# A three-layer decoder kernel on one core: a new order of the steps around each batch boundary

## What is computed

```python
x = _layernorm(x + _L0_attn_ref(x, ...))                      # no mask; aperture and expression gates
x = _layernorm(x + _L0_xattn_ref(x, ctx, ctx, mask, ...))     # keys and values from ctx, with a mask
x = _layernorm(x + _L0_ffn_ref(x, ...))                       # 16 experts with causal attention
# both attentions, in short, for every head:
scores = (x @ Wq) @ (kv @ Wk).T / sqrt(32)     # 1024 x 1024; masked: -1e9 where mask == 0
out    = softmax(scores) @ (kv @ Wv)
y      = concat(heads of out) @ Wo
```

## Time and profile before

| | |
|---|---|
| Median of 3 runs | 4500.99 us (4493.58 to 4504.22) |
| The profiled execution | 4493.35 us, span 4491.5 us, mean granted TensorE clock 0.964 |
| Span of the two attentions | to about 3512 us |
| Third layer | 3512 to 4491 us |
| PE / DVE / POOL / ACT busy | 4094.5 / 2557.7 / 1800.2 / 1704.6 us |

### The profile page before, as it was taken

One profiled execution on the slowest core, in us unless ns is written; L12 is line 12 of the kernel. 1 busy time (PEld: TensorE's weight loads), 2 busy tenths in 40 slices (PEclk: granted clock), 3 DMA queues, 4 the chain that ended last, 5 costly groups with the idle time before them and its releaser, 6 DMA issues. The chain is left out here.

```text
span 4491.5 us, 65447 instructions
## 1 busy us (share of the span) xinstructions
PE 4094.5 (91%) x20596; PEld 2374.2 (53%) x20596; DVE 2557.7 (57%) x4092; ACT 1704.6 (38%) x3114; POOL 1800.2 (40%) x1263
## 2 busy tenths in 40 slices
PE   4899989989999999899989988998998599999998
PEld 3543744364446436443644364436443477777776
DVE  2564456446534655576567566756674555565554
ACT  1355145425443553344234424442444322222222
POOL 2223122222241224476357535754664244444343
PEclk8999999999998999999999999999999799999998
DMA  2321232132213224322422333223220300000000
GB/s 82 73 50 48 71 93 59 53 85 65 56 51 94 52 62 150 85 43 72 141 67 43 90 127 76 53 94 119 57 43 20 139 27 27 27 29 30 29 29 12
DMA packets 136375, 294.68 MB, mean 66 GB/s; under 512 B 19856, under 2 KB 37904, under 8 KB 136016
## 3 DMA queue, kind: packets, MB, share of 16 engines
q1 hardware_dynamic: 125520, 272.93, 22.5%
q10 hardware_dynamic: 10496, 17.31, 1.1%
HBM read 145.74 MB, written 43.25 MB: 42 GB/s over the span
## 5 line engine op out<-in xcount | busy, mean ns | idle before, releaser
L1133 ACT ACTIVATE probs_a<-half_a 128x512 f32<-128x512 f32 x2048 | 1120.8, 595 | 976.7 <-PE half_a L934 451.0
L931 PE MATMUL half_a<-stack_a 97*128 97x512 f32 x2048 | 874.0, 485 | 75.1 <-DMA stack_a<-mrow_a 36.5
L1369 DVE TENSOR_REDUCE mx_a<-wide_a 128x1 f32<-128x1024 f32 x512 | 601.3, 1219 | 548.3 <-PE wide_a L890 542.3
L1365 DVE CUSTOM_DVE_ANT_0 wide_a<-wide_a,mask_q_a 128x1024 f32<-128x1024 f32 x512 | 619.5, 1245 | 289.3 <-PE wide_a L890 278.4
L890 PE MATMUL wide_a<-stack_a 96*128 96x512 f32 x2048 | 674.3, 438 | 61.3 <-DVE mx_a L1369 31.0
L931 PEld LDWEIGHTS half_a<-stack_a 97*128 97x128 f32 x2048 | 377.3, 194 | 633.1 <-ACT probs_a L1133 326.3
L779 POOL TENSOR_TENSOR psums_a<-psums_a,probs_a 128x1024 f32<-128x1024 f32 x232 | 559.7, 2432 | 144.2 <-ACT probs_a L1133 121.3
L1758 PE MATMUL work_e<-w_in_e,x_e 128*128 128x512 f32 x2304 | 573.9, 401 | 17.7 <-DVEq L2014 10.3
L873 PE MATMUL acc_a<-probs_a,v_a 128*32 128x512 f32 x4096 | 553.0, 610 | 3.1 <-ACT u_a L1104 3.0
L890 PEld LDWEIGHTS wide_a<-stack_a 96*128 96x128 f32 x2048 | 386.0, 196 | 230.7 <-DVE mx_a L1369 57.0
L1758 PEld LDWEIGHTS work_e<-w_in_e,x_e 128*128 128x128 f32 x2304 | 429.7, 191 | 119.4 <-issue 20.3
(11 more groups left out here) (238 smaller groups left out, 4558.9 us busy)
## 6 DMA issues: line engine op xcount, KB each, us to landing
stack_a<-qk_a SPq DMA_DIRECT2D x336, 256.0 KB, 4.9
y_a<-x SPq DMA_DIRECT2D x8, 2048.0 KB, 8.8
x<-y_a SPq DMA_DIRECT2D x8, 2048.0 KB, 7.5
mstage_a<-mask SPq DMA_DIRECT2D x32, 512.0 KB, 4.3
mstage_a<-mask_t SPq DMA_DIRECT2D x32, 512.0 KB, 4.1
stage_a<-x_t SPq DMA_DIRECT2D x24, 512.0 KB, 3.7
stack_a<-first_a SPq DMA_DIRECT2D x48, 256.0 KB, 5.0
x_t<-xts_late_a ACTq DMA_DIRECT2D x10, 1024.0 KB, 7.6
```

The costliest lines, as they stand in the source:

```text
L931: last = pe.matmul(bank[:, :], stack[0:3 * DH + 1, s, 2 + h, kt * P:(kt + 1) * P], stack[0:3 * DH + 1, s, h, c * CH:(c + 1) * CH], start=T ...
L1133: act.activation(probs[:, kt % 2 * 2 + h, c * CH:(c + 1) * CH], bank[:, :], ACT.Exp, scale=SCALE).then_inc(free, 1)
L1365: dve.tensor_tensor_reduce(bank[:, :], bank[:, :], mask_q[:, t, :], 1.0, -3e38, ALU.add, ALU.max, mx[:, p % 3, n:n + 1]).then_inc(free, 1)
L1369: dve.tensor_reduce(mx[:, p % 3, n:n + 1], bank[:, :], AX.X, ALU.max).then_inc(free, 1)
```

## The change

Six edits, all to the order of the steps and to one helper of TensorE:

- `MAXIMA`: no maxima in tile 0 of pair 0; the row becomes 0, 2, 3, 3, 3, 3, 3, 2 (19 instead of 21), and pair 4 gets 3 instead of 2 in tiles 6 and 7.
- `mneg` of a pair is put behind the first two `st` of the next tile, in front of that tile's maxima, where it stood behind the tile's last `st`. In pair 5 it comes at the end of the tile in which the sixteenth maximum stands.
- The masked section's key masks 8 to 15 leave V (one per V tile) and go two at a time behind K(0,0), K(1,0), K(2,0), K(3,0).
- The last pair's norm steps in the masked section: steps 0; 1 and 2; 3 and 4; 5 and 6 behind V tiles 0, 1, 2, 3 instead of one behind each of tiles 1 to 7 (counted from 0, step n behind tile n + 1).
- `with_maxima`: of a unit's maxima all but one stand in front of it, the unit is cut in two halves of 6 matmuls (a step `part` for the first), and the last one stands between them.
- The order of K and Q units and of the transposes around `mneg` 0 changes: the two blocks of the diff with `xt[:2]` and with `xt[:HALF]` are for a next batch with the mask and without it.

```diff
-MAXIMA = ((2, 3, 3, 3, 3, 3, 2, 2),) + ((2,) * 8,) * 4 + ((2, 3, 3, 3, 3, 3, 1, 0), (2, 2, 2, 2, 1, 0, 0, 0), (0,) * 8)
+MAXIMA = ((0, 2, 3, 3, 3, 3, 3, 2),) + ((2,) * 8,) * 3 + ((2, 2, 2, 2, 2, 2, 3, 3),) + ((2, 3, 3, 3, 3, 3, 1, 0), (2, 2, 2, 2, 1, 0, 0, 0), (0,) * 8)
...
-            steps += [("st", p, kt, 0, c) for c in range(NC_)]
-            misc = due
+            steps += [("st", p, kt, 0, c) for c in range(NC_)] + due
...
-                steps += [units_[0], ("st", p, kt, 1, 0), units_[1], ("st", p, kt, 1, 1)] + misc
+                steps += [units_[0], ("st", p, kt, 1, 0), units_[1], ("st", p, kt, 1, 1)]
             else:
-                steps += units_ + [("st", p, kt, 1, c) for c in range(NC_)] + misc
+                steps += units_ + [("st", p, kt, 1, c) for c in range(NC_)]
...
             steps += [("pv", *before, part) for part in parts] + late
+            if p == 5:
+                steps += due
+                due = []
...
-def mask_places():
-
-    place = {("pv", n): n for n in range(4)}
-    place.update({("V", 3 + n): 4 + n for n in range(5)})
-    place.update({("out", 1 + 2 * n): 9 + n for n in range(4)})
-    place.update({("K", n): 13 + n for n in range(3)})
+def mask_places(att):
+
+    if att == 1:
+        return {("K", n // 2): (TT + n, 2) for n in range(0, TT, 2)}
+    place = {("V", 3 + n): (4 + n, 1) for n in range(5)}
+    place.update({("out", 1 + 2 * n): (9 + n, 1) for n in range(4)})
+    place.update({("K", n): (13 + n, 1) for n in range(3)})
...
     def masks(kind, n):
 
-        if change and (kind, n) in mask_at:
-            m = mask_at[kind, n]
-            return [("mask", m)] + ([("mload", m + 2)] if m + 2 < 2 * TT else [])
-        return []
+        if nxt != 1 or (kind, n) not in mask_at:
+            return []
+        from_, count = mask_at[kind, n]
+        return [step for m in range(from_, from_ + count)
+                for step in [("mask", m)] + ([("mload", m + 2)] if m + 2 < 2 * TT else [])]
 
     def with_maxima(units, rates):
 
         out = []
         for unit, rate in zip(units, rates):
-            out.extend(unit)
-            out.extend(first[:rate])
-            del first[:rate]
+            out += first[:rate - 1]
+            del first[:rate - 1]
+            out.append(("part", *unit))
+            out.append(first.pop(0))
+            out.append(unit)
         return out
...
-            tail[n + 1].append(("norm", PAIRS - 1, n))
+            tail[(n + 1) // 2 + (1 if att == 0 else 0)].append(("norm", PAIRS - 1, n))
...
-            if att == 1:
-                steps += [("mask", TT + t)] + ([("mload", TT + t + 2)] if t < TT - 2 else [])
...
-            steps += [("Q", 0, 0), ("Q", 1, 0), ("Q", 0, 1), ("stack", 0)] + xt[:HALF] + [("Q", 1, 1)]
-            fill = [[("Q", 2, 0)], [("Q", 2, 1)], [("Q", 3, 0)], [("Q", 3, 1)], xt[HALF:HALF + 2], xt[HALF + 2:]]
-            last = [("CS", n) for n in range(4)]
+            steps += [("Q", 0, 0)] + xt[:2] + [("Q", 0, 1), ("stack", 0), ("Q", 1, 0), ("Q", 1, 1)] + xt[2:HALF]
+            steps += with_maxima([("Q", g, c) for g in (2, 3) for c in range(NC_)], (4, 3, 3, 3))
+            steps += first + [("CS", n) for n in range(4)] + xt[HALF:HALF + 2]
+            steps += [("mneg", 0), ("stack", 1)] + xt[HALF + 2:]
...
-            ks = [[(kind, g, c)] for kind, g in (("K", 0), ("K", 1), ("Q", 0), ("Q", 1)) for c in range(NC_)]
+            ks = [[(kind, g, c)] for kind, g in (("K", 0), ("K", 1), ("Q", 0)) for c in range(NC_)]
...
-            fill = [[("K", 2, 0)], [("K", 2, 1), ("Q", 2, 0)], [("Q", 2, 1), ("K", 3, 0)], [("K", 3, 1), ("Q", 3, 0)],
-                    [("Q", 3, 1)], xt[:2]]
-            last = xt[2:]
-        steps += with_maxima(fill, (3, 3, 3, 3, 2, 2))
-        assert not first
-        steps += [("mneg", 0), ("stack", 1)] + last
+            steps += [("K", 2, 0), ("K", 2, 1), ("K", 3, 0)]
+            fill = [("K", 3, 1)] + [("Q", g, c) for g in (1, 2, 3) for c in range(NC_)]
+            steps += with_maxima(fill, (3, 3, 2, 2, 2, 2, 2))
+            steps += first + xt[:HALF] + [("mneg", 0), ("stack", 1)] + xt[HALF:]
...
-                for k in range(KT):
+                for k in tiles:
...
+                    begun = kind != "part" and ("part", *step) in sec.steps
+                    tiles = range(KT)
+                    if kind == "part":
+                        step = step[1:]
+                        kind = step[0]
+                        tiles = range(KT // 2)
+                    elif begun:
+                        tiles = range(KT // 2, KT)
...
-                    if not half_ring.opens(sec, step):
+                    if not begun and not half_ring.opens(sec, step):
...
-                                     lambda k: x_lo[:, k, c * CH:(c + 1) * CH])
+                                     lambda k: x_lo[:, k, c * CH:(c + 1) * CH], tiles)
+                        if tiles == range(KT // 2):
+                            continue
```

More of the change, by code:

```diff
@@ L124, in section_steps @@
     first = [("sm", 0, h, t) for h in range(2) for t in range(TT)]
-    change = att == 0 and nxt == 1
-    mask_at = mask_places()
+    mask_at = mask_places(att)
     def masks(kind, n):
-        if change and (kind, n) in mask_at:
-            m = mask_at[kind, n]
-            return [("mask", m)] + ([("mload", m + 2)] if m + 2 < 2 * TT else [])
-        return []
+        if nxt != 1 or (kind, n) not in mask_at:
[3 more added lines that the diff above has]
+                for step in [("mask", m)] + ([("mload", m + 2)] if m + 2 < 2 * TT else [])]
     def with_maxima(units, rates):
@@ L825, in _, with parts @@
             pe.wait_ge(const_in, 16 * CONSTS)
-            def parts(out, hi_l, lo_l, hi_r, lo_r):
-                for k in range(KT):
+            def parts(out, hi_l, lo_l, hi_r, lo_r, tiles=range(KT)):
+                for k in tiles:
                     for n, (a, b) in enumerate(((hi_l, hi_r), (hi_l, lo_r), (lo_l, hi_r))):
```

## The result

The changed kernel takes 4522.0 us (median of 5 runs, 4519.5 to 4525.2), the kernel before beside it on the same chip 4497.4 (4489.4 to 4504.2). The ratio is 1.0054, with a 95% interval of 1.0043 to 1.0065: **24 us slower** (19 to 29). The forecast was 4491 (10 us faster), the range ended at 4520, and slower had a chance of 0.23, mostly by a mechanism that did not occur.

What follows compares the result with a forecast made beforehand. TensorE, busy 91% of the span, was taken as the bound, with idle time at batch boundaries. Terms summed to -10.1 us: 4483.3 against the profiled execution, 4491 against the median; range 4466 to 4520.

Steps and rivals of the forecast that it cites:

- halves: Four boundaries to an unmasked batch: half units between maxima remove TensorE's waits for VectorE; -19.7 us (-26 to -12).
- norms: V of three masked passes: earlier norm product lets out start at once and K 5.7 us earlier; -17.1 us.
- masks in K: K of three masked passes: mask loads delay VectorE, K(2,1) waits 5 to 7.5 us for its bank; +23.4 us.
- Q order: Four boundaries to a masked batch: saved and new waits nearly cancel, -0.5 each; -2 us (-8 to +8).
- row in front, with pair 5: Inside pairs: second maximum waits for mneg's copy, old mneg and row waits go; +10.8, -5.3 and -10 us.
- maxima out of tile 0: Pair 0's start and pair 4: moved maxima cost pair time, 0.95 and 1.5 a batch; +9.8 us (3 to 16).
- the rates: Maxima per tile in pairs 0 and 4, the same term as maxima out of tile 0; +9.8 us.
- the first (waits hidden): K: VectorE's waits for the masks are hidden, so the +23.4 vanishes; 4467 us, chance 0.15.
- the second (row late at the next pair's st): Pair starts: the row of maxima lands after the next pair's first st; 4515 us, chance 0.2.
- The third (gains given back): Boundaries: gains go into stack landing and slow clock behind them, half of -19.7 lost; 4501 us, chance 0.23.

Runs made afterwards that it cites:

- run 3: Kernel before with only the projections cut in halves at the four boundaries to an unmasked batch; ratio 0.996, -18 us.
- run 7: Kernel before with only the norm steps moved, two per V tile; ratio 0.9981, -8.5 us.
- run 1: Kernel before with only the key mask's second half moved from V, two at a time behind K(0,0) to K(3,0); ratio 1.0056, +25 us.
- run 8: Changed kernel with the masks put back in V, one per tile; ratio 0.9963 against the kernel before, -17 us.
- run 2: Kernel before with only the new order of Q, transposes, maxima and CS at boundaries to a masked batch; ratio 1.0013, +6 us.
- run 5: Kernel before with the row of maxima in front and pair 5's mneg at tile 6's end, but old maxima per tile; ratio 0.9988, -5.4 us.
- run 4: Kernel before with all changes inside the pairs: row in front, maxima out of tile 0, pair 5's mneg; ratio 1.0048, +22 us.
- run 9: Changed kernel with masks back in V and the old maxima per tile in pairs 0 and 4; ratio 0.9923 against the kernel before, -35 us.
- run 12: Kernel before with row in front and pair 5's mneg, pair 0's tile 0 empty, three maxima in tiles 1 to 7, pair 4 unchanged; 1.002, +9 us.
- run 13: Changed kernel, masks still in K but spread so K(0,1)'s low half follows mask 11, queries' loads behind K(1,1); 1.0073 against before, +33 us.
- run 14: Kernel before with the changed kernel's Q order, but all transposes ahead of mneg and CS behind it; ratio 1.0009, +4 us.
- run 10: Kernel before with projections in halves at unmasked boundaries, norms two per V tile, pair 5's mneg earlier in unmasked batches; 0.9931, -31 us.

## Why the prediction was wrong, step by step

Each term of the sum beside what it measured, moved alone:

| step | predicted | measured | run |
|---|---|---|---|
| halves | -19.7 (-26 to -12) | -18 | 3 |
| norms | -17.1 | -8.5 | 7 |
| masks in K | +23.4 | +25 alone, +41 in place | 1, 8 |
| Q order | -2 (-8 to +8) | +6 | 2 |
| row in front, with pair 5 (+10.8 - 5.3 - 10) | -4.5 | -5.4 | 5 |
| maxima out of tile 0 | +9.8 (3 to 16) | +27 | 4, 5 |
| sum | -10.1 | +26 (changed kernel: +24) | |

The measured parts, each with some 4 to 7 us to either side, add up to the whole, but partly by luck, for they are not independent: without the masks the parts give +1, some 11 to either side, and run 8 measured -17 (-22 to -11). Taken out of the changed kernel one after the other (runs 8 and 9), the account is another and has no remainder: the masks +41 for 23.4, the rates +18 for 9.8, all the rest -35 for -43.3. That is 17.5, 8 and 9 of the 34 us between -10 and +24. Which step failed most depends on the base, masks or maxima; both were priced at far too little.

**Maxima out of tile 0** failed most of the parts moved alone: 17 of the 36 us between -10 and +26, and over the end of its bounds. I priced the two maxima as work ("They now cost 1 us of pair time, less one that ran in the slow stretch"). They were filler, which kept TensorE busy while ScalarE loaded its table and made the first exps. Without them TensorE idles 0.9 to 2.4 us more in the first 12 us of a batch, and in the masked batches the clock stays at the lower level besides: 0.57 to 0.68 for 0.81 to 0.86 (runs 4, 5, 12). My own showed a wait followed by a unit in 4.43 us for 2.9; I used it for the boundary and not for the pair's start. The empty tile is some 16 us of it. Pair 4 takes 1.2 us more unmasked and 1.8 masked, its two more maxima included. Pairs 1 and 2 take 7 over the eight batches, which I had put at nothing.

**Norms.** "K starts 5.7 earlier" is wrong: 3.0 in the changed kernel (from the load's issue to K 53.7 us before, 50.7 now), and 2.3 in run 7. I let POOL be done "probably sooner" than 2606.7; it was done at the same 21.7 us behind the load. The additions, with one split behind them, let out begin 2.6 earlier, less than the 3.77 that I had taken as the least. That POOL's pace then holds out was right, and out itself became no shorter to speak of. I also missed that the masks' leaving V makes the same product early: beside it the norms' move gained nothing up to out (run 1).

**Masks in K.** Kind and place were right: VectorE in order, K(2,1), three times, then the slow clock. Sizes: I had 5 to 7.5 us of wait and 7.8 a boundary, it was 9.1 to 9.9 and 12.6. The three rounds took 5.6 us each, not 4.5 to 5.3, for a load landed in 4.4 us and not in 3.6 (two of them were now under way at a time), and masks 8 and 9 took 3.26 together. What I mentioned and gave no price is the real bound: the queries' load behind mask 15 (run 13). That my 23.4 is so near the +25 of the part alone is luck: the boundaries cost 41 to 44 (runs 8 and 1), and V gave back some 9, which I had put at nothing ("where V's pace hid them"). In the changed kernel, where the norms have already taken most of that, 2.8 comes back.

**Q order.** My -0.5 doesn't follow from the terms that stand ahead of it. Inside the one boundary cut above it came out so (53.76 us for 53.88), the xt wait of "some 3.2" was 2.8 to 3.2 in run 2 and 1.9 to 2.8 in the changed kernel, and mneg 0 waits no more for the clamp. What failed is that I looked no further than mneg: of the moved transposes I did not follow the DMA that ScalarE issues to the start of the loop's next pass behind it, though I did so at the unmasked boundary. At the boundary near 2730 it stands like this, ScalarE then TensorE's third st:

```profile
2733.37 0.39 ACTq L1165 DMA_DIRECT2D x_t<-xts_late_a  x1
2739.23 1.28 ACT L1145 ACT_TABLE_LOAD   x1 [6.19 <-issue]
```

```profile
2741.17 0.79 PE L941 MATMUL half_a<-stack_a 97*128 97x512 f32 x1 [4.65 <-ACT probs_a L1145]
```

**Right:** the halves as a whole (the 6.5 at the first loop boundary was 3.3 in the changed kernel, since a 1 MB issue took 3.6 us ahead of mneg's copy, and the first batch gave 7 in place of 4); the row in front with pair 5, where 0.6 us of wait for the copy was 0.17 and the 19.3 of mneg came back elsewhere, about evenly. The unmasked wait for the row in pair 5 went as said. **Rivals:** the first (waits hidden) and the second (row late at the next pair's st) did not occur, the row's waits fell to 7; the second's 0.2 was most of my chance for slower, so the 0.23 that I gave to it is no merit. The Trainium skill ("DMA: Bandwidth & Descriptors", "Issuing engines are not separate DMA queues") says that the transfers of ScalarE and SP interleave on the same engines. The 4.8 of the earlier trace rows agrees, with stack transfers of SP's queue under way, for the 1.8 that is the median; run 14's 7.3 us is no test of it, since the 1 MB ahead of that row is on the row's own queue. Both are rows at pair 0, not, as I had it, at the pairs behind it. The third (gains given back) named the right mechanism, slow clock behind a wait, but only for the gains.

## What to carry to other kernels

Work that fills another engine's start-up wait is worth more than its own duration: before moving it, ask what TensorE does in its place, and price the clock of the matmuls behind it too. When a step is moved, follow every DMA that it issues to the next thing that its queue or engine owes (here the start of the loop's next pass, an 8 KB row behind 1 MB). Parts measured alone can add up to the whole by luck: take them out of the whole as well. And cost a chain through a small buffer to its last user, not to the first that waits: relieving the first only moves the wait.

## What was unexpected of the hardware

- TensorE's busy time is no constant: the same 20596 matmuls took 4075.0 us (run 10) to 4117.0 (run 13), 42 us apart; the granted clock over the span was 0.968 in the one and 0.958 in the other. Lists of waits miss this; in run 4 the lines that changed rose by 3.5 us together and the time by 22.
- ScalarE's issue of a 1 MB DMA took 0.4 to 4.0 us. Where the loop's next pass began behind it, ScalarE's table load followed its end by 5.5 us or more (5.5 to 6.5 in run 2); at the loop's end by 0.5 to 0.7.
- An 8 KB DMA issued 0.8 us behind a 1 MB one on the same queue landed in 7.3 us, one issued 6 us behind it in 4.8, the median one in 1.8.
- A 512 KB mask load landed in 3.6 us at one place and in 4.4 where two were under way at a time.
